# Seven value projections moved behind the head chain, one block for projections and self-attention, and the rows' normalisation on GpSimd

## The reference, cut to what matters

```
xn = layernorm(layernorm(x)) * ln_gamma + ln_beta
q, k, v = heads(xn @ w_q.T), heads(xn @ w_k.T), heads(xn @ w_v.T)
qn = q / rms(q) * q_gamma * 64**-0.5       # rms over a head's 64 columns
kn = k / rms(k) * k_gamma
attn = softmax(qn @ kn.T)                  # 2048 x 2048 for each head
x = x + (attn @ v) @ w_o.T + b_o
```

## Time and profile before

| | before |
|---|---|
| median of 3 runs | 2325.62 us (2323.33 to 2331.70) |
| profiled execution | 2321.48 us |
| its span | 2319.6 us |
| TensorE busy | 2189.6 us (94%) |
| VectorE busy | 1565.5 us (67%) |
| ScalarE busy | 1609.7 us (69%) |
| GpSimd busy | 1483.9 us (64%) |
| mean granted TensorE clock | 0.982 |

### The profile page before, as it was taken

How to read it: one execution, slowest core, us unless ns; L and a number is a source line. 1 busy time by engine, 2 the same in 40 slices (tenths; PEclk the granted TensorE clock), 3 DMA queues, 4 the chain that set the end, 5 groups by cost and what they waited for, 6 DMA issues and landing times. The chain is left out here.

```text
span 2319.6 us, 63272 instructions
## 1 busy us (share of the span) xinstructions
PE 2189.6 (94%) x22392; PEld 1256.9 (54%) x22392; DVE 1565.5 (67%) x2601; ACT 1609.7 (69%) x1831; POOL 1483.9 (64%) x980
## 2 busy tenths in 40 slices
PE   6998999999997989899999899999999978998999
PEld 3544666666665445444445446666666644554444
DVE  6987777777776756753379877777777766667532
ACT  4555999999998556731145579999999975566210
POOL 4324998989988577731233158898998976867210
PEclk9998999999999999999999989999999999999999
DMA  4210000000001301102122100000000022011000
GB/s 105 64 37 5 2 9 9 9 9 9 9 0 29 105 1 38 46 15 77 46 55 58 34 1 10 0 9 9 9 9 9 4 63 67 1 47 37 19 22 34
DMA packets 102338, 65.10 MB, mean 28 GB/s; under 512 B 75346, under 2 KB 75346, under 8 KB 102226
## 3 DMA queue, kind: packets, MB, share of 16 engines
q1 hardware_dynamic: 102226, 63.57, 12.3%
HBM read 46.69 MB, written 8.39 MB: 24 GB/s over the span
## 5 line engine op out<-in xcount | busy, mean ns | idle before, releaser
L751 POOL TENSOR_TENSOR probs_l<-wide 128x1024 f16<-128x1024 f32 x448 | 986.3, 2234 | 162.3 <-PE bank L803 120.7
L887 DVE TENSOR_REDUCE pm<-bank 128x1 f32<-128x512 f32 x1024 | 680.5, 688 | 249.1 <-PE bank L759 244.2
L878 ACT ACTIVATE wide<-bank,shift 128x1024 f32<-128x1024 f32 x512 | 570.4, 1114 | 37.3 <-DVE probs_l L901 30.7
L870 ACT ACTIVATE wide<-bank,shift 128x1024 f16<-128x1024 f32 x512 | 567.6, 1109 | 10.9 <-PE bank L775 10.9
L759 PE MATMUL bank<-ko,q_hh 128*128 (+1 forms) x1024 | 397.0, 390 | 22.3 <-PEq L454 12.2
L774 PE MATMUL bank<-q_hh,ko 128*128 (+1 forms) x1024 | 389.9, 381 | 18.1 <-ACT wide L878 13.1
L775 PE MATMUL bank<-q_lm,k_h 65*128 (+1 forms) x1024 | 389.8, 381 | 0.0
L788 PEld LDWEIGHTS bank<-v_hl,wide 128*128 128x128 f16 x4096 | 287.5, 98 | 63.4 <-issue 5.7
L788 PE MATMUL bank<-v_hl,wide 128*128 (+1 forms) x4096 | 319.8, 192 | 0.1
L790 PE MATMUL bank<-v_hl,wide 128*128 (+1 forms) x4096 | 318.0, 193 | 0.0
L790 PEld LDWEIGHTS bank<-v_hl,wide 128*128 128x128 f16 x4096 | 267.4, 96 | 58.7
(11 more groups left out here) (211 smaller groups left out, 4187.5 us busy)
## 6 DMA issues: line engine op xcount, KB each, us to landing
wide<-in_x SPq DMA_DIRECT2D x32, 256.0 KB, 2.6
q_lm<-in_x SPq DMA_DIRECT2D x32, 256.0 KB, 3.2
ko<-in_L_ffn_W SPq DMA_DIRECT2D x32, 256.0 KB, 3.8
q_hh<-q_hh SPq DMA_DIRECT2D x32, 128.0 KB, 2.6
ko<-k_h SPq DMA_DIRECT2D x32, 128.0 KB, 2.8
out<-bo_b SPq DMA_DIRECT2D x16, 256.0 KB, 2.0
out<-xbo_b SPq DMA_DIRECT2D x16, 256.0 KB, 2.0
q_lm<-nm SPq DMA_DIRECT2D x248, 0.2 KB, 4.9
```

Source lines behind the costliest of these rows:

```text
L751: pool.tensor_tensor(probs_l[:, p % 2, :], probs[:, p % 2, :], probs_h[:, p % 4, :], ALU.subtract).then_inc(pl_pool, 1)
L870: act.activation(probs_h[:, p % 4, :], SB[p % 2][:, :], ACT.Exp, bias=shift[:, 0:1]).then_inc(ph_ready, 1)
L878: act.activation(probs[:, p % 2, :], SB[p % 2][:, :], ACT.Exp, bias=shift[:, 0:1]).then_inc(p_ready, 1)
L887: dve.tensor_reduce(pm[:, s, k:k + 1], MB[k % 2], AX_X, ALU.max).then_inc(mx_free, 1)
```

## The change

- The two blocks of a batch become one. The small buffers of self-attention move into sq, its low probabilities into qkn. Waits stand where the block's end was: TensorE before its first maximum waits for the last heads' low parts and for all head copies (a_dup); GpSimd's two memsets wait for the last sum of squares and for the last value product (a_v_done).
- `over_tiles` goes: the 16 steps are written out.
- `row_normalise` is called by GpSimd, between the scale and the affine, no longer by VectorE.
- Tiles 9 to 15 (LATE = 7) have no v in their step. Their rows' high and low parts are kept in the space of v_hl that their own values will take. Their 84 products follow behind step 15, alternately into banks 7 and 2: tiles 9 and 10, the last head transposes, tiles 11 and 12, and then two products behind each of the first 18 maxima (tiles 13 to 15).
- ScalarE's high and VectorE's low parts of these values follow at the places shown. The exponential's table is loaded before them.

```diff
@@ projections, setup
+                    LATE = 7
+                    FIRST_LATE = KB - LATE
+                    late = [v_hl[:, t * (H * VW):t * (H * VW) + 2 * D].rearrange("p (s n) -> p s n", s=2)
+                            for t in range(KB)]
+                    eye16 = sq[:, 0:P // 2].bitcast(F16)
+                    probs_l = qkn[:, :, :].rearrange("p s n -> p (s n)").bitcast(F16).rearrange("p (s n) -> p s n", s=2)
+                    def turned(t):
+                        return (late[t][:, 0, :], late[t][:, 1, :]) if t >= FIRST_LATE else \
+                            (rows_h[:, t % 2, :], rows_l[:, t % 2, :])
+                    def v_bank(t):
+                        return banks[2] if t >= FIRST_LATE and (t - FIRST_LATE) % 2 else banks[7]
-                    def over_tiles(eng, step):
...
@@ sync
-                        sp.wait_ge(a_dup, (b + 1) * (32 * KB))
@@ gpsimd
                                 row_scale(pool, b, t + 2, s)
+                                row_normalise(pool, b, t + 2, s)
                                 row_affine(pool, b, t + 2, s)
...
-                        over_tiles(pool, step)
+                        for t in range(KB):
+                            step(t, t % 2, t > 0, t + 1 < KB, t + 2 < KB)
+                        pool.wait_ge(a_ssq, (T0 + KB) * 2 + 1)
                         pool.memset(nm0[:, :, :], 0.0).then_inc(e_zero, 1)
+                        pool.wait_ge(a_v_done, T0 + KB)
                         pool.memset(v_hl[:, :].rearrange("p (k e) -> p k e", e=VW)[:, :, DH:DH + 1], 1.0)\
                             .then_inc(a_ones, 1)
@@ tensor
+                        def late_values(first, last):
+                            for i in range(first, last):
+                                t, d, kind = FIRST_LATE + i // (3 * DC), i // 3 % DC, i % 3
+                                if i % (3 * DC) == 0:
+                                    pe.wait_ge(a_v_ready, T0 + t + (1 if t == FIRST_LATE else 0))
+                                xh, xl = turned(t)
+                                mm = pe.matmul(v_bank(t)[:, :], (xl if kind == 2 else xh)[:, d * P:(d + 1) * P],
+                                               (wl if kind == 1 else wh)["v"][:, d, :], start=(i % (3 * DC) == 0),
+                                               stop=(i % (3 * DC) == 3 * DC - 1))
+                                if i % (3 * DC) == 3 * DC - 1:
+                                    mm.then_inc(a_v_done, 1)
...
-                            pe.wait_ge(a_v_ready, T0 + t + 1)
-                            project(s, "v", VB, a_v_done)
+                            if t < FIRST_LATE:
+                                pe.wait_ge(a_v_ready, T0 + t + 1)
+                                project(t, "v", v_bank(t), a_v_done)
...
+                        V = 3 * DC
+                        late_values(0, 2 * V)
                         head_transposes(KB - 1)
+                        late_values(2 * V, 4 * V)
+                        pe.wait_ge(a_ht_free, (T0 + KB) * 2 + 2)
+                        pe.wait_ge(a_dup, (b + 1) * (32 * KB))
...
-                        for k in range(16):
-                            unit_max(0, k)
-                        for k in range(2):
-                            unit_max(1, k)
+                        for k in range(18):
+                            unit_max(k // 16, k % 16)
+                            late_values(4 * V + 2 * k, 4 * V + 2 * k + 2)
...
                         pe.wait_ge(a_ones, 2 * b + 2)
+                        pe.wait_ge(a_v_ready, T0 + KB + 1)
                         scores(0, 0, fresh=True)
@@ scalar, after the steps
                         act.preload_act_table(ACT.Exp)
+                        v_high(FIRST_LATE)
+                        v_high(FIRST_LATE + 1)
+                        heads_high(KB - 1)
+                        for t in range(FIRST_LATE + 2, KB):
+                            v_high(t)
@@ vector, step and after the steps
                                 row_low(dve, b, t + 1, *turned(t + 1))
-                            if next2:
-                                row_normalise(dve, b, t + 2, s)
...
+                        v_low(FIRST_LATE)
+                        v_low(FIRST_LATE + 1)
+                        heads_low(KB - 1)
+                        v_low(FIRST_LATE + 2)
                         dve.tensor_copy(eye16[:, :], ident[:, :]).then_inc(e_eye, 1)
+                        v_low(FIRST_LATE + 3)
                         for k in range(16):
                             reduce_max(0, k, 0)
+                            if k in (7, 13):
+                                v_low(FIRST_LATE + (4 if k == 7 else 5))
                         dve.wait_ge(e_zero, b + 1)
                         negate_max(0, 0)
                         for k in range(AHEAD):
+                            if k == 2:
+                                v_low(KB - 1)
                             reduce_max(1, k, 1)
```

More of the change, by code:

```diff
@@ L468, in decoder_layer @@
                     KBK = banks[5:7]
-                    VB = banks[7]
-                    block = ph.enter_context(nc.Block())
-                    T0 = b * KB
-                    def over_tiles(eng, step):
[L478 to L486, removed]
+                    SB = pairs[0:2]
@@ L506, in _ @@
                             if t + 6 < KB:
-                                load_x(t + 6, t % 2)
-                        sp.wait_ge(a_dup, (b + 1) * (32 * KB))
[L509 to L521, removed]
-                            if next2:
-                                row_scale(pool, b, t + 2, s)
-                                row_affine(pool, b, t + 2, s)
-                            if not before:
-                                ones()
-                        over_tiles(pool, step)
@@ new lines, in head_transposes @@
+                        def head_transposes(t):
+                            for which in range(2):
+                                pe.wait_ge(a_qk, (T0 + t) * 2 + which + 3)
+                                pe.wait_ge(a_ht_free, (T0 + t) * 2 + which + 1)
+                                for d in range(DC):
+                                    mm = pe.transpose(HT[which][:, d * P:(d + 1) * P],
+                                                      qkn[:, which, d * P:(d + 1) * P], ident[:, :])
+                                mm.then_inc(a_ht_done, 1)
@@ L862, in _, with square, root @@
                     def _(act):
-                        act.preload_act_table(ACT.Exp)
+                        def square(t, which, bank, done):
+                            act.wait_ge(done, T0 + t + 1)
+                            act.wait_ge(a_ssq, (T0 + t) * 2 + which + 1)
+                            act.activation(sq[:, :], bank[:, :], ACT.Square, scale=INV_WS).then_inc(a_sq, 1)
+                        def root(t):
+                            act.wait_ge(a_ssq, (T0 + t) * 2 + 3)
+                            act.activation(ms[:, :], ssq[:, :], ACT.Sqrt, scale=WS * WS / DH).then_inc(a_ms, 1)
@@ new lines, in v_high, with step @@
+                        def v_high(t):
+                            act.wait_ge(a_v_done, T0 + t + 1)
+                            act.activation(v_tile(t, False), v_bank(t)[:, :].rearrange("p (h d) -> p h d", d=DH), ACT.Copy,
+                                           scale=INV_WS).then_inc(a_vh, 1)
+                        def step(t, s, before, next1, next2):
+                            square(t, 0, QB[s], a_q_done)
+                            if next1:
+                                row_high(act, b, t + 1, turned(t + 1)[0])
+                            square(t, 1, KBK[s], a_k_done)
+                            if before:
+                                heads_high(t - 1)
+                            root(t)
+                            if t < FIRST_LATE:
+                                v_high(t)
```

310 lines of the change are left out of this document (146 added, 164 removed).

## The result

The changed kernel takes 2320.54 us (median of 20 executions, one of them an outlier of 12301.49; the others 2315.0 to 2323.3), the kernel before 2328.23 (20, 2323.3 to 2334.2). The ratio is 0.9964 [0.9954, 0.9973]: 0.36% faster, some 8 us, less than half of the 16.8 forecast. The profiled execution took 2315.09 (span 2313.3), 6.4 less than that of before; its page has TensorE busy 2178.3 us, VectorE 1552.2, ScalarE 1612.0, GpSimd 1542.5.

A forecast was written before the change was run, and what follows sets the result against it. TensorE was taken to bound the projections at 9.08 us a step, VectorE close behind. Batch 0's -8.0 and batch 1's -8.8 make -16.8 us, taking the 2325.62 median to 2308.8, stated as 2308; range 2299 to 2319.

The forecast's parts named there:

- Normalisation on GpSimd: Rows' normalisation moved from VectorE, taken as 1.27 us on GpSimd (bounds 0.43 and 2.54); hidden in steady steps.
- step 2: Where TensorE waits for rows behind GpSimd's ones' memset; two normalisations of 1.35 on that chain cost +1.3 us a batch.
- late steps: Steps 9 to 15 without value products: mostly 7.7 us each by a walk of the waits, -9.6 us a batch.
- the two sums of the table: Changes per batch up to the first exponential: forecast -8.0 and -8.8 us, measured -1.6 and -4.4.
- Steps 3 to 8: Steps set by TensorE, claimed to stay at 9.08 us, with nothing gained by relieving VectorE.
- S15 to the first reduction: From VectorE's last scaling (S is a tile's scaling end), values 9 to 12 round the last head transposes: -0.5 us.
- First reduction to first exponential: Values 13 to 15 between the maxima, products fitting in at full clock: +0.8 us in batch 0, 0 in batch 1.
- Straight code and one block: Loops written out set at 0 (at most 2 us a batch); removed block end worth no more than the -0.5.
- B: Rival: GpSimd's normalisation is slow, 2.54 us, costing step 2 and late steps 11 us in all: 2319; chance with A 0.20.
- A: Rival: another exposed joint in the heads' chain holds late steps near 8.5 us, 11 in all: 2319; chance with B 0.20.
- C: Rival: TensorE falls to half clock before the maxima, +7.6 us a batch: 2341, slower; chance 0.06.
- D: Rival: nothing gained, VectorE's queue at the maxima taking back 8 us a batch: 2326; chance 0.06.

The follow-up runs named there:

- e2_ones_late: The changed kernel with GpSimd's memset of the ones moved behind step 15, normalisation still on GpSimd: 2307.52 us, ratio 0.991.
- e5_no_maximum: The changed kernel without VectorE's maximum (lower bound on the mean square), the reciprocal reading ms: 2314.94 us, ratio 0.9949.
- e6_no_late_values: The changed kernel without deferred values (LATE = 0) and with the normalisation on VectorE: 2326.51 us, ratio 0.9997.
- e1_norm_vector: The changed kernel with the rows' normalisation back on VectorE: 2304.77 us, ratio 0.9891.
- nine against ten: The changed kernel with normalisation on VectorE and the ones' memset beside the maxima (2301.35 us), against e10_before_ones_maxima (2320.39 us): 0.992.
- e10_before_ones_maxima: The kernel before with only GpSimd's memset of the ones moved beside the second block's maxima: 2320.39 us, ratio 0.9977.
- experiments 1, 4, 5 and 6: e1_norm_vector; e6_no_late_values; the changed kernel, normalisation on VectorE, ones' memset behind step 15, 2314.24 us; the kernel before, memset behind step 15, 2328.27 us.

## Why the prediction was wrong

**The step that failed** is "Normalisation on GpSimd", in the sentence "I take one such pass, 1.27, the same engine, shape and type". It lasts 2.08. The bounds (0.43 and 2.54) held it, and the nearest row was the wrong one: a pass with two inputs and one operation says nothing of one with two operations and a value for each row. By the prediction's own steps the 0.8 us more take back, in both batches together, 3.0 us in step 2 and some 2.6 in the late steps, as the chain over GpSimd then permits 7.95 a step where the walk had 7.7: over half of the 10.8 by which the two sums of the table fall short. The rest is the clock and the held maxima. In detail:

- Step 2: two normalisations of 2.08 where 0.71 and 0.66 of waiting stood, +2.8 instead of +1.3. Batch 1 has +2.9. Batch 0 has +4.9: 0.7 for tile 2 (the wait of 0.80), +1.9 for tile 3, +1.7 for the half clock behind that wait, and 0.56 before the transposes of tile 1, where it ran longer at half clock; no cause was looked for. The clock behind the wait was the term left out: the earlier trace rows shows that 1.80 us of idle lengthens only the transposes behind it; at 3.69 the products of the next 3 us ran at 0.51. Batch 1 of the same trace would have warned, with half clock behind 2.09 us; since it had paid this before, it lost only the 2.9. e2_ones_late takes the wait away and the clock is 1.00 in 43 to 52.
- Late steps: the chain over two steps was put at 15.1, 7.6 a step. With 0.8 more for the normalisation it permits 8.0, and e5_no_maximum, which has no maximum to be held, has 8.07 in the mean. The maximum held for 0.6 in each chain gives the other 0.33: 8.40. From one end of scaling to the next it is 8.4 in the four steps 10 to 13 and 7.81 in step 14, where 7.7 and 7.45 were forecast: 3.1 us with the small differences, and -9.6 becomes -6.5. (The walk has a slip of 0.1: S8 = 107.2 and a step of 8.45 give 115.65.)

**What no step had:** VectorE's maximum held behind GpSimd. It was to be read in two rows of the trace of before (0.75 and 0.94 where 0.17 and, in the changed kernel, 0.22 are the free durations). It costs the change about 2 us a batch in the late steps, and it leaves the kernel before a doubtful base: its profiled execution lost nothing at the memset, others may have, so the 4.1 us from it to the median can't be taken as a constant offset. The page "GPSIMD Engine Reference" of the Trainium skill, section "4.1 Engine selection", puts one-input work at about line rate. The trace does not agree: 1.57 us for one operation and 2.08 for two, where VectorE needs 0.54. The measurement decides.

**The steps that held.** Steps 3 to 8 at 9.08; GpSimd's length hidden there. The first late step, S8 to S9, at 8.49 for 8.45, and the last at 6.79 for 6.7. S15 to the first reduction -0.5, to the digit. First reduction to first exponential +0.5 and -0.3 for +0.8 and 0; the products fit between the maxima at full clock. Straight code and one block: nothing (e6_no_late_values). The late steps do give nearly 9.6 when nothing stands in their way: 63.97 to 54.6 is -9.4 in e1_norm_vector, and two batches of it make nearly all of the 19 us of nine against ten. There VectorE does the normalisation too, and the step is 7.89 where 7.7 + 0.46 = 8.16 would follow: the gaps that I counted on VectorE were some 0.3 too many. That -9.4 comes so near to -9.6 is therefore in part luck: the normalisation that VectorE still has there makes up for gaps that it does not have. This didn't show in the change as made, where the chain over GpSimd sets the step.

**The rivals.** B had the mechanism and nearly the size: 2319 by 2.54 us, measured 2320.5 with 2.08 and the two terms it did not have, the clock and the held maxima. A would show late steps at 8.5 for a joint among the heads' buffers; the steps are 8.4, but e5_no_maximum and the waits for GpSimd's rows show the cause, so A is refuted in spite of its number. C is refuted for its place (1.00 in 167 to 193), though half clock did come, behind the wait in step 2. D is refuted: the maxima took back 0.5 us in batch 0 and nothing in batch 1.

**Open.** From the first exponential of batch 1 to the end the first two profiled executions last 973.9 (before) and 974.2 (after), the ten others 976.4 to 979.2, in code that no edit touches. The tables by stretches show where: the granted clock is lower. In the stretch from 600 to 660 us behind that exponential it is 0.97 in the first two (1945.66 to 2005.66 in the kernel before) and 0.89 to 0.94 in the ten others (0.89 in e10_before_ones_maxima, 1939.11 to 1999.11). Why it is lower there is open. So differences of 4 us between two profiled executions say nothing by themselves; the verdicts rest on ratios over several executions, and the traces only on the marks before it.

## What to carry to other kernels

Moving work to an idle engine needs that engine's price for the same form (operations, operands, a value for each row), not for the same shape; and where the engine stands in a chain, slack in its busy share says nothing. When the mean of a small VectorE operation is several times its shortest, look at what GpSimd ran at its end: it is a wait written as work, and a long one-partition memset belongs where VectorE has only reductions or PSUM reads. A kernel whose executions spread by 0.5% may have a race of order within it, or a clock that falls in some of them; look for it first, since it moves the base that every change is measured against.

## What was not expected of the hardware

- VectorE's 128x16 maximum of 0.17 us was held 6.80, 7.00, 6.17 and 5.15 us by a GpSimd memset on one partition (experiments 1, 4, 5 and 6), and 0.75 beside an affine pass; its 128x128 cast took 0.94 where it ended with the second of two GpSimd memsets, 0.35 in e10_before_ones_maxima where it ended with the first, and 0.22 with none beside it. The reductions, the low parts (which read PSUM), the statistics and, beside an affine pass, the reciprocal were not held.
- GpSimd's tensor_scalar over 128x512: 1.57, 1.93 and 2.08 us by its form; two passes with two inputs need 1.27 each.
- A wait of 3.69 us of TensorE in the middle of dense work brought 3 us at half clock behind it (0.51 in 47 to 50); one of 2.09 was followed by half clock too (0.68 in 1193 to 1198 of the kernel before); one of 1.80 was not.
